# One-hot rows and radial basis made four groups ahead in the edge loop of a graph network kernel

## The reference, cut to what matters

```python
rbf = exp(-0.5 * ((w[:, None] - centers) / (|widths| + 1e-5)) ** 2) * env(w)[:, None]     # 64 per edge
r   = silu(rbf @ rbf_w1 + rbf_b1) @ rbf_w2 + rbf_b2
W   = silu(silu(r @ filt_w1 + filt_b1) @ filt_w2 + filt_b2) @ filt_w3 + filt_b3           # 256 per edge
msg = (x[dst] @ node_w + node_b) * W
h   = x + segment_sum(msg, src)         # then layer norm, gate, norm, and the second layer
```

## Time and profile before

| what | us |
|---|---|
| median of 3 runs (5696.37 to 5717.07) | 5700.58 |
| the profiled execution | 5722.47 |
| its span, from the first to the last instruction | 5720.7 |
| PE busy in it | 3678.5 (64%) |
| POOL busy | 3435.5 (60%) |
| DVE busy | 2387.8 (42%) |
| ACT busy | 1607.6 (28%) |

### The profile page before, as it was taken

How to read it: one execution, slowest core, us unless ns; L and a number is a source line. 1 busy time by engine, 2 the same in 40 slices (tenths; PEclk the granted TensorE clock), 3 DMA queues, 4 the chain that set the end, 5 groups by cost and what they waited for, 6 DMA issues and landing times. The chain is left out here.

```text
span 5720.7 us, 76061 instructions
## 1 busy us (share of the span) xinstructions
PE 3678.5 (64%) x16356; PEld 2722.4 (48%) x16357; DVE 2387.8 (42%) x7105; ACT 1607.6 (28%) x4212; POOL 3435.5 (60%) x3664
## 2 busy tenths in 40 slices
PE   7888888888888888888998433333332454444443
PEld 5555555555555555555887323222222444444443
DVE  5444444444444444443326322122212654545557
ACT  4444343444434434344666211111110000000000
POOL 2655555655555656565764666666666566666665
PEclk8888889888888988899999666665655777776776
DMA  7333333333333333334994111111112333333324
GB/s 221 110 107 106 108 109 106 109 107 105 109 109 105 108 106 110 106 110 146 297 293 135 54 43 44 45 43 43 44 44 60 101 86 87 84 82 86 87 79 91
DMA packets 460153, 590.18 MB, mean 103 GB/s; under 512 B 65456, under 2 KB 380848, under 8 KB 460080
## 3 DMA queue, kind: packets, MB, share of 16 engines
q0 software_dynamic: 128512, 318.04, 18.3%
q1 hardware_dynamic: 331584, 271.50, 16.8%
HBM read 392.61 MB, written 197.07 MB: 103 GB/s over the span
## 5 line engine op out<-in xcount | busy, mean ns | idle before, releaser
L533 POOL DMA_INDIRECT s_rows<-arena,adr x784 | 790.0, 1008 | 809.5 <-issue 765.9
L573 POOL DMA_INDIRECT d_rows<-arena,adr x832 | 810.0, 974 | 503.7 <-issue 250.0
L586 POOL DMA_INDIRECT arena<-x_half,idx x832 | 801.7, 964 | 503.4 <-issue 227.8
L525 POOL DMA_INDIRECT arena<-y_rows,idx x784 | 757.3, 966 | 306.0 <-issue 238.2
L987 PE MATMUL ps<-f3s,arena 128*128 128x256 f32 x3136 | 878.2, 442 | 40.5 <-issue 40.4
L1375 DVE TENSOR_TENSOR arena<-arena,ps 128x512 f32<-128x512 f32 x392 | 268.0, 689 | 1354.0 <-remote 611.7
L987 PEld LDWEIGHTS ps<-f3s,arena 128*128 128x128 f32 x3136 | 720.7, 230 | 185.3 <-issue 47.9
L1164 PE MATMUL ps<-arena 128*128 128x128 f32 x1664 | 372.3, 393 | 663.3 <-DVE arena L1557 586.8
L976 PE MATMUL ps<-arena,f2s 128*128 128x512 f32 x1568 | 732.2, 611 | 30.9 <-ACT arena L640 29.2
L1164 PEld LDWEIGHTS ps<-arena 128*128 128x128 f32 x1664 | 321.1, 288 | 704.9 <-issue 703.9
L647 ACT ACTIVATE arena<-ps,col 128x512 f32<-128x512 f32 x392 | 268.1, 684 | 1009.1 <-PE ps L976 840.5
(11 more groups left out here) (217 smaller groups left out, 5444.2 us busy)
## 6 DMA issues: line engine op xcount, KB each, us to landing
arena<-s_rows SPq DMA_DIRECT2D x104, 1048.0 KB, 5.7
arena<-d_rows SPq DMA_DIRECT2D x52, 1040.0 KB
arena<-de_rows SPq DMA_DIRECT2D x392, 128.0 KB
d_rows<-arena,adr POOLq DMA_INDIRECT x832
arena<-x_half,idx POOLq DMA_INDIRECT x832
s_rows<-tpl_s SPq DMA_DIRECT2D x98, 131.0 KB
arena<-y_rows,idx POOLq DMA_INDIRECT x784
s_rows<-arena,adr POOLq DMA_INDIRECT x784
```

Source lines behind the costliest of these rows:

```text
L525: pool.indirect_dma_start(gath[b][:, t, :], None, y_rows, bass.IndirectOffsetOnAxis(ap=idx[b][:, t:t + 1], axis=0)).then_inc(gathered[b], 16)
L533: pool.indirect_dma_start(s_rows, bass.IndirectOffsetOnAxis(ap=adr[b][:, t:t + 1], axis=0), msg[b][:, t, :], None).then_inc(scattered[b], 16)
L573: pool.indirect_dma_start(d_rows, bass.IndirectOffsetOnAxis(ap=adr2[b][:, t:t + 1], axis=0), drow[b][:, t, :], None).then_inc(scattered_d[ ...
L586: pool.indirect_dma_start(gath2[b][:, t, :], None, x1_half, bass.IndirectOffsetOnAxis(ap=idx2[b][:, t:t + 1], axis=0)).then_inc(gathered2[ ...
```

## The change

Four things are changed, and the work on data stays the same.

1. The rings `rbf` and `hot_r` hold four groups, not two.
2. DVE makes `radial_basis` and `one_hot_rank` of group g+4 in turn g (before: g+2 and g+3), and ACT makes `radial` of g+4 (before: g+3). The first four of each are made ahead of the loop.
3. DVE takes `product(g+2)` first in its turn, then the messages of g-1, then `ranked(g+2)`, and the two steps for g+4 last.
4. ACT's `radial` waits for `rbf_done` of two groups before, since `th` still has two buffers.

The order on PE, POOL and SP is the same.

```diff
-        rbf = [take(GW) for _ in range(2)]
+        rbf = [take(GW) for _ in range(4)]
-        hot_r = [take(GT, NB2, dt=bf16) for _ in range(2)]
+        hot_r = [take(GT, NB2, dt=bf16) for _ in range(4)]
...
+                if not (fixed(g) and g < 2):
+                    act.wait_ge(rbf_done, g - 1)
                 A(sq, de[b][:, 0, :], ACT.Square, bias=negc[:, 0:1]).then_inc(squared, 1)
...
-                if ahead(g, 3):
-                    radial(g + 3, q + (b + 3) // 4, (b + 3) % 4)
                 if ahead(g, 4):
+                    radial(g + 4, q + 1, b)
                     stage_idx(g + 4, q + 1, b)
...
             def one_hot_rank(g, b):
-                if not (fixed(g) and g < 2):
-                    dve.wait_ge(rank_mm, g)
+                if not (fixed(g) and g < 4):
+                    dve.wait_ge(rank_mm, g - 2)
...
-                if not (fixed(g) and g < 2):
-                    dve.wait_ge(l1_mm, g - 1)
+                if not (fixed(g) and g < 4):
+                    dve.wait_ge(l1_mm, g - 3)
...
             def dve_group(g, q, b):
                 if ahead(g, 2):
-                    radial_basis(g + 2, b + 2)
+                    product(g + 2, b + 2)
                 if not (fixed(g) and g == 0):
                     for h in range(2):
                         messages(g - 1, q + (b + 3) // 4 - 1, (b + 3) % 4, h)
                 if ahead(g, 2):
-                    product(g + 2, b)
                     ranked(g + 2, b)
-                if ahead(g, 3):
-                    one_hot_rank(g + 3, b + 1)
+                if ahead(g, 4):
+                    radial_basis(g + 4, b + 4)
+                    one_hot_rank(g + 4, b + 4)
...
-            one_hot_rank(2, 2)
+            for g in range(2, 4):
+                radial_basis(g, g)
+                one_hot_rank(g, g)
```

More of the change, by code:

```diff
@@ L698, in _ @@
             radial(2, 0, 2)
+            radial(3, 0, 3)
             loop(act, act_group, G0, 4, 4, 4)
@@ L937, in rank_step @@
                 pe.wait_ge(hot_done, g + 1)
-                cur, prev = hot_r[b % 2], hot_r[1 - b % 2]
+                cur, prev = hot_r[b % 4], hot_r[(b + 3) % 4]
                 if not (fixed(g) and g == 0):
@@ L958, in layer1 @@
                 pe.wait_ge(rbf_done, g + 1)
-                mm(ps[:, 0, 0:GW], w1d[:, :], rbf[b % 2], start=True, stop=True).then_inc(l1_mm, 1)
+                mm(ps[:, 0, 0:GW], w1d[:, :], rbf[b % 4], start=True, stop=True).then_inc(l1_mm, 1)
             def layer23(g, b):
@@ L996, in pe_group @@
                 if ahead(g, 2):
-                    rank_step(g + 2, b)
-                    layer1(g + 2, b)
+                    rank_step(g + 2, b + 2)
+                    layer1(g + 2, b + 2)
                 if not (fixed(g) and g == 0):
@@ L1313, in one_hot_rank @@
             def one_hot_rank(g, b):
-                if not (fixed(g) and g < 2):
-                    dve.wait_ge(rank_mm, g)
+                if not (fixed(g) and g < 4):
+                    dve.wait_ge(rank_mm, g - 2)
                 for t in range(GT):
                     for f in range(2):
-                        last = V.tensor_scalar(hot_r[b % 2][:, t, f * NB:(f + 1) * NB], lane[:, 0:NB],
+                        last = V.tensor_scalar(hot_r[b % 4][:, t, f * NB:(f + 1) * NB], lane[:, 0:NB],
                                                blk2[:, bass.ds(g * GT + t, 1), f], None, ALU.is_equal)
@@ L1325, in product @@
                     dve.wait_ge(rank_done, g)
-                V.tensor_tensor(prod[:, :, :], hot_r[b % 2], ps[:, 7, 0:GT * NB2].rearrange("p (t n) -> p t n", t=GT),
+                V.tensor_tensor(prod[:, :, :], hot_r[b % 4], ps[:, 7, 0:GT * NB2].rearrange("p (t n) -> p t n", t=GT),
                                 ALU.mult).then_inc(prod_done, 1)
@@ L1364, in radial_basis @@
                 dve.wait_ge(rbf_chain, 2 * g + 2)
-                if not (fixed(g) and g < 2):
-                    dve.wait_ge(l1_mm, g - 1)
-                V.scalar_tensor_tensor(rbf[b % 2], rcp, -0.5, de[b % 4][:, 1, :], ALU.add, ALU.mult).then_inc(rbf_done, 1)
+                if not (fixed(g) and g < 4):
+                    dve.wait_ge(l1_mm, g - 3)
+                V.scalar_tensor_tensor(rbf[b % 4], rcp, -0.5, de[b % 4][:, 1, :], ALU.add, ALU.mult).then_inc(rbf_done, 1)
             def messages(g, q, b, h):
```

## The result

| | us |
|---|---|
| before, median of 7 runs (5691.98 to 5717.07) | 5700.98 |
| after, median of 7 runs (5728.1 to 5745.26) | 5733.49 |
| after, the profiled execution | 5732.1 |
| its span | 5730.3 |

The changed kernel takes 1.0056 of the time before, 95% interval 1.0045 to 1.0068: slower by 32 us, just over the bound of 0.5%. The prediction was 5710, with 5660 to 5760 for its likeliest case, so it foresaw some 9 us where 32 came.

What follows compares the result with a forecast made beforehand. A ring through POOL, 13.32 us a turn, was taken as the bound. Profiled 5722.5 plus 20 gave 5742, less 22 for the median 5720; 5710 was taken as the middle of 5660 to 5760, within an outer range of 5360 to 5860.

Steps and rivals of the forecast that it cites:

- likeliest case: Whole kernel: edge loop at 12.9 to 13.4 us a group, 5660 to 5760 us in all; chance 0.45.
- The ring through POOL: Edge loop: message 0.69, hand-over 1.02, eight transfers 10.07, count seen 1.54, together 13.32 us; removing PE's waits gains nothing.
- Early count, seam, standstill: Edge loop: layer5's count at F + 6.1, POOL's next scatter without a pause, then POOL idle 5.68 us a turn later.
- F: Start of a group's second message on DVE, from which the prediction counts times in a turn; 1516.70 in its example.
- pairs: Edge loop: two turns joined without a pause plus the idle time after them, 26.1 us, 13.05 a group.
- locked turn: Edge loop: a turn whose layer5 count doesn't come early, put at 13.3 us as before the change.
- let go together: DVE: product and message released at once by late PE counts, message 0.6 us later; bounds 0 to 0.6, taken as 0.
- The 13.2: Edge loop: forecast mean us a group, (26.1 + 2 x 13.3) / 4, against 13.10 before; +0.1, 20 us.
- Gathers that land in SBUF hold the counts: Edge loop: PE's counts are held up while POOL's gathers land, and seen 1.5 to 1.6 us behind them.
- Product first costs nothing: DVE's turn: moving product ahead of the messages costs 0, bounds 0 and 0.6 us a turn.
- The rival "faster": Edge loop: counts not held as long, or standstill not tied to POOL's seam; 10.4 us, 5175 at best, 5465 halfway; chance 0.27.
- The rival "slower": Edge loop: standstill catches layer4's count, layer5 not begun; pair 28.8 us, 5955, or 5855 mixed; chance 0.24.

Runs made afterwards that it cites:

- Pause: Kernel after, with POOL waiting after its four gathers until they have landed before the next scatter; 1.0098 of before on chip A, 5703.99 us.
- only ahead: Kernel after with DVE's product moved back behind the messages; ratio 0.9998 on chip B, 1.0054 on chip C.
- outward transfers: Each gather from group 4 on replaced by an indirect transfer out of SBUF; 1.0083 on the kernel after, 0.9999 on the one before.
- two halves: Kernel before with product ahead of the messages, and kernel after with product back behind them; 1.0043 and 0.9998 on chip B.

## Why the prediction was right, and where it was not

**The ring through POOL: right.** PE's two waits were 2.0 us a turn, and the clock came with them; all were taken away, and the loop got no faster where counts are held. The price that the text gave for their removal, nothing, holds. The text chose PE as the busiest engine by the busy share of its matmuls, 64%. The section it names (the Trainium skill, Perfetto Trace Analysis, Identifying the Most-Contended Engine) wants TensorE's headroom judged by its useful work or by the busy share of its weight loads instead. The profile has the weight loads (PEld) busy 48%, under POOL's 60%, so by that measure POOL comes first, as in the rows.

**Early count, seam, standstill: right, and free of net cost.** One cycle in the changed kernel's timeline goes nearly as written:

```profile
1541.94 0.69 DVE L1377 TENSOR_TENSOR arena<-arena,ps 128x512 f32<-128x512 f32 x1 [5.05 <-remote]
...
1543.26 3.72 PE L989 MATMUL ps<-f3s,arena 128*128 128x256 f32 x16 [1.73 <-ACT ps L670]
...
1547.31 1.27 DVE L1377 TENSOR_TENSOR arena<-arena,ps 128x512 f32<-128x512 f32 x2
...
1553.87 1.00 POOL L533 DMA_INDIRECT s_rows<-arena,adr  x1 [0.31 <-issue]
```

From F = 1541.94 the next messages start at F + 5.4, before the gathers begin at 1548.79; the prediction had the count at F + 6.1. The path of PE was another than the text added up, though. Rank_step and layer1 were done before F, and layer5 waited only for ACT's bias and started at 1543.26, F + 1.3, not F + 2.45. POOL then runs into its next scatters without a pause and pays in the turn after. Seams went from 11 to 45, a mix of pairs with about two locked turns each, as the text had it. "Pause" shows the link from the other side: no seam, no standstill.

**The price of the locked turn: the term that was too small.** The pauses over 5 us after the change last up to 6.5 us, 5.8 in the mean, near the 5.68 used, and a pair takes 2 x (10.02 + 2.95) = 25.9 us where the sum had 26.1. The locked turn was put at 13.3, as before the change. It takes 10.02 + 3.73 = 13.75, because both counts of layer5 are now held in most of these turns. With the other pauses left at 3.11, the same seams would have made the kernel slightly faster. The text had a bound of 0.6 us a turn for "let go together", but for the product with the message; "only ahead" has the same long turns without it. For the two messages with each other it had no term.

**The 13.2: in part luck.** The measured mean over the loop is 13.22, yet the terms don't add up to it. The prices 13.05 and 13.3 were read in the middle of the loop, and they were held against 13.10, the mean over all of it. That mean is lower because the last three turns of the loop have no gathers and take 5 to 7 us (from 400 to 2600 us the kernel before takes 13.24). By its own prices the mix of 13.2 was no loss at all. The value that was recorded, 5710, stands 9 us above before where 32 came, and "faster" had the highest of the three chances, 0.40. The range holds the result; the size of the change was missed.

**Gathers that land in SBUF hold the counts: wrong.** The outward transfers hold them as well, on both kernels, and so do transfers of 64 bytes a row, and, for up to 2.3 us, scatters when there are no gathers at all. What the runs leave is POOL's indirect transfers themselves: other work of POOL and full DMA queues hold nothing. It made no difference to the sum, because gathers and scatters come one behind the other; but it was the wrong thing to test for. It also overturns one argument on the way, that rank_step's count is safe while POOL is at its scatters: the product waited up to 14.3 us. With the messages behind it that could have been costly. It wasn't, since layer5's counts were held in the same stretch.

**Product first costs nothing: wrong by a little, and in both directions.** Alone it gains 0.56% on chip C and costs 0.43% on chip B; on top of the look-ahead it is worth 1.0063 against 1.0054, no difference.

**The rival "faster" was true of another chip.** Its condition, counts that aren't held, its 10.4 us and POOL's constant 0.30 are what chip B shows. But there the kernel before takes 4680, as "only ahead" does with its 10.17 us a group, so its time for the change (5175) was wrong in any case: where its condition holds there is nothing left to gain. The changed kernel as a whole was not run on chip B; the product of the two halves is about 1.004 there, an estimate.

**The rival "slower"** had a pair of 28.8 us because layer4's count is caught too, which makes a pause of 8.4. Turns with a late layer4 exist (10.15 us before layer4 in the chip C turn; 16 such waits from 1000 to 2000 us of the kernel after), but through layer23's count, not layer4's. They don't lengthen the standstill: the longest is 6.5 us in the kernel after and 7.0 in its run on chip C.

**Still open.** Which part of POOL's work on an indirect transfer holds the counts, whether only the count or the matmul's write too is late, why layer5's own matmuls creep at 2.1 to 2.8 us in such a stretch, and why both counts of layer5 are held more often after the change. Every kernel here keeps its four scatters of 1 KB rows, so it isn't shown that small transfers alone would hold. Each chip was measured once, in one sitting, so it isn't shown that chip B's prompt counts belong to the chip.

## What to carry to other kernels

Before taking away the waits of the busiest engine, look from what each consumer's start is counted: here messages started 1.5 us behind POOL's last transfer, whether layer5 had ended 3.8 or 0.9 us before. A gap that is released from outside the engine's own chain can be emptied without effect, and work that comes early can cost nothing in its own turn and lengthen the turns around it. And run a change of half a per cent on more than one chip: the same edit, product first, was worth -0.56% on one and +0.43% on another.

## What the hardware showed that I had not expected

- The kernel before takes 5644 to 5703 us on chips A and C and 4680 on chip B. The edge loop is 13.1 us a group on the chip of the result and 10.2 to 10.3 in the two halves on chip B, with matmuls of 379 ns (median) and indirect transfers of 0.95 to 1.00 us on both. Nearly all of the difference lies in stages with indirect transfers of POOL. The granted clock from 1000 to 1600 us was 1.00 in "only ahead" on chip B and 0.88 in it on chip C, where PE often waits.
- Counts of PE are held while POOL runs through its indirect transfers, up to 14.3 us by the longest wait in the kernel after, and come 1.5 us after the last one (2.6 to 3.1 after a run of two turns without a pause). The hold isn't complete: single counts get through in such a stretch, one at 1507.14 in the turn shown. The records of the updates show them posted late, on chip B within 0.02 us.
- For the second four transfers of a turn neither the direction nor the bytes matter: 1 KB a row inward, 1 KB outward and 64 bytes outward do the same. POOL busy with comparisons for 253 of 360 us, beside 294 GB/s of other transfers, delays none of 792 counts.
- With a wait on POOL for its own gathers, in front of the next scatter, POOL's pause is 2.8 to 4.1 us in every turn.
